# Skip projection of the nodes moved from the node stage into the edge stage, with a new order of the second norm and the sum with x

## The reference

```
h    = relu(layernorm(x))
z    = layernorm(h) * ln1_g + ln1_b
q, k, v = z @ Wq.T + bq, z @ Wk.T + bk, z @ Wv.T + bv        (4 heads of 32)
e    = edge_attr @ We.T
a    = softmax over the edges of one target of (q[dst] . (k[src] + e)) / sqrt(32)
out  = segment_sum(a * (v[src] + e), dst)
skip = z @ Wskip.T + bskip                                   (one row per node)
beta = sigmoid([out, skip, out - skip] @ Wbeta.T)
x_l  = h + beta * skip + (1 - beta) * out
h2   = layernorm(x_l) * ln2_g + ln2_b
x1   = x + x_l + relu(h2 @ W1.T + b1) @ W2.T + b2            (hidden width 512)
```

## Time and profile before

| | us |
|---|---|
| median of 3 runs | 3551.7 |
| the profiled execution, its own time | 3547.84 |
| its span, first to last instruction | 3546.1 |
| mean granted TensorE clock (1.00 is 2.4 GHz) | 0.837 |
| busy: TensorE / VectorE / ScalarE / GpSimd | 2276.2 / 2282.9 / 1725.3 / 2351.8 |

### The profile page before, as it was taken

One profiled execution on the slowest core, in us unless ns is written; L12 is line 12 of the kernel. 1 busy time (PEld: TensorE's weight loads), 2 busy tenths in 40 slices (PEclk: granted clock), 3 DMA queues, 4 the chain that ended last, 5 costly groups with the idle time before them and its releaser, 6 DMA issues. The chain is left out here.

```text
span 3546.1 us, 56764 instructions
## 1 busy us (share of the span) xinstructions
PE 2276.2 (64%) x13730; PEld 1826.3 (52%) x13730; DVE 2282.9 (64%) x9173; ACT 1725.3 (49%) x4075; POOL 2351.8 (66%) x2429
## 2 busy tenths in 40 slices
PE   0002887877877774799999999996444343455554
PEld 0002777777766672566666666664333332444444
DVE  8886666666666664678878878884111111677777
ACT  8994233332333332588888888885111111343433
POOL 5554777777777771665565556562777775777776
PEclk9999999999999995899999999998555555555555
DMA  6553233333333332233333434441666664556676
GB/s 204 177 177 94 83 101 91 91 101 91 91 101 92 91 101 63 70 109 102 111 106 102 106 104 108 101 104 67 130 131 128 132 130 103 130 142 146 145 153 124
DMA packets 253889, 401.94 MB, mean 113 GB/s; under 512 B 56515, under 2 KB 165456, under 8 KB 253728
## 3 DMA queue, kind: packets, MB, share of 16 engines
q1 hardware_dynamic: 183670, 265.77, 25.5%
q0 software_dynamic: 63424, 133.57, 19.7%
q10 hardware_dynamic: 6682, 1.46, 0.3%
HBM read 241.74 MB, written 160.29 MB: 113 GB/s over the span
## 5 line engine op out<-in xcount | busy, mean ns | idle before, releaser
L1159 POOL DMA_INDIRECT agg<-rows,at_n x392 | 393.8, 1005 | 149.6 <-issue 116.3
L1657 POOL DMA_INDIRECT aggc<-rows,at_nc x392 | 406.1, 1036 | 113.2 <-issue 104.8
L628 POOL DMA_INDIRECT zs<-z_table,at_s x392 | 381.3, 973 | 112.9 <-issue 102.5
L628 POOL DMA_INDIRECT zd<-z_table,at_d x392 | 374.0, 954 | 119.4 <-issue 110.9
L1482 POOL DMA_INDIRECT h2s<-h_table,at_s x392 | 373.3, 952 | 113.2 <-issue 90.2
L1535 PE MATMUL p_sum<-h2s,same 128*128 128x129 f32 x784 | 206.3, 439 | 310.8 <-DMA h2s<-h_table,at_s 206.6
L1233 PE MATMUL p_f<-w_t,act 128*128 128x128 f32 x3136 | 383.8, 278 | 0.0
L1222 PE MATMUL p_f<-z_t,w_t 128*128 128x512 f32 x784 | 374.9, 612 | 4.3 <-ACT act L1294 4.1
L1233 PEld LDWEIGHTS p_f<-w_t,act 128*128 128x128 f32 x3136 | 361.2, 192 | 22.2 <-issue 22.2
L1535 PEld LDWEIGHTS p_sum<-h2s,same 128*128 128x128 f32 x784 | 174.6, 323 | 342.4 <-issue 275.3
L1522 DVE TENSOR_SCALAR same<-dst_sb,dst_g 128x128 f32<-128x128 uint16 x392 | 83.9, 302 | 404.1 <-DMA dst_sb<-dst 370.5
(11 more groups left out here) (317 smaller groups left out, 6444.7 us busy)
## 6 DMA issues: line engine op xcount, KB each, us to landing
rows<-rows_sb SPq DMA_DIRECT2D x49, 576.0 KB
h_table<-h2b SPq DMA_DIRECT2D x49, 516.0 KB, 2.9
rows<-rows_sb SPq DMA_DIRECT2D x49, 516.0 KB
xa<-in_x_dram SPq DMA_DIRECT2D x49, 512.0 KB, 3.7
z_table<-za SPq DMA_DIRECT2D x49, 512.0 KB, 2.9
dst_sb<-dst SPq DMA_DIRECT2D x98, 256.0 KB
xb<-in_x_dram SPq DMA_DIRECT2D x49, 512.0 KB, 4.0
x_table<-x1b SPq DMA_DIRECT2D x49, 512.0 KB
```

The source lines that it names most:

```text
L628: pool.indirect_dma_start(out=to[:, slot, k], out_offset=None, in_=z_table, in_offset=bass.IndirectOffsetOnAxis(ap=at[:, slot, k:k + 1], a ...
L1159: pool.indirect_dma_start(out=agg[:, ring, k], out_offset=None, in_=rows0, in_offset=bass.IndirectOffsetOnAxis(ap=at_n[:, ring, k:k + 1], ...
L1657: pool.indirect_dma_start(out=agg[:, slot, k], out_offset=None, in_=rows1, in_offset=bass.IndirectOffsetOnAxis(ap=at_n[:, slot, k:k + 1], ...
```

## The change

The projection leaves the node stage. The edge stage loads 8 tiles of z rows of nodes per step (`zn`), turns them in pairs (bank p_tr[1]; the gathered rows share p_tr[0] alone), multiplies by wsk_t in the bank of v (p_v), copies the result out and stores it in `skip_table`. The node stage loads it with x. In the banks that come free the node stage has two for z2 and four for f1. The prep chain (den, recip, wa_sum, now with one logit add) moves behind norm2 on VectorE; x_xl moves behind norm2 too; the eighth tile of z2 goes from ScalarE to VectorE; gate_exp and the copies of z2 come first on ScalarE, and h2 and h are in another order. The diff, cut to its core:

```
@@ edge stage, SyncE @@
                         if new:
                             g, slot, use = new
+                            at_least(sp, node_turned, 4 * (g - 1))
+                            hold(sp, held)
+                            rows = z_table[bass.ds(first_row(g), GR), :].rearrange("(p t) d -> p t d", t=G)
+                            sp.dma_start(zn[:, slot], rows).then_inc(zn_in[slot], 16)
                             at_least(sp, same_ready, 4 * (g - 1))
...
                             sp.dma_start(rows, rows_sb[:, slot]).then_inc(stored[slot], 16)
+                            if isinstance(g, int) and g == NGN - 1:
+                                sp.wait_ge(skip_out[1 - slot], 16 * ((g - 1) // 2 + 1))
+                            sp.wait_ge(skip_kept, 4 * g + 4)
+                            hold(sp, held)
+                            rows = skip_table[bass.ds(first_row(g), GR), :].rearrange("(p t) d -> p t d", t=G)
+                            sp.dma_start(rows, skip_sb[:, slot]).then_inc(skip_out[slot], 16)
@@ edge stage, TensorE @@
+                    def turn_nodes(g, slot, use, n):
+                        if n == 0:
+                            pe.wait_ge(zn_in[slot], 16 * (use + 1))
+                        at_least(pe, node_copied, 4 * g + n)
+                        hold(pe, held)
+                        for k in range(2):
+                            last = t_.transpose(p_tr[1][:, k * P:(k + 1) * P], zn[:, slot, 2 * n + k], ident[:])
+                        last.then_inc(node_turned, 1)
+
+                    def skips(g, slot, use, n):
+                        pe.wait_ge(node_copied, 4 * g + n + 1)
+                        pe.wait_ge(v_copied, 4 * g + n + 1)
+                        hold(pe, held)
+                        for k in range(2):
+                            last = t_.matmul(p_skip[:, k * (D + 1):(k + 1) * (D + 1)], zn_t[:, n % 2, k], wsk_t[:], start=True, stop=True)
+                        last.then_inc(node_skipped, 1)
 # turn:
-                        at_least(pe, z_copied, 4 * g + u - 1)
+                        at_least(pe, z_copied, 4 * g + u)
 # project, before the value part:
+                        at_least(pe, skip_kept, 4 * g + u)
 # half:
                         if new:
+                            turn_nodes(*new, 0)
                             turn(*new, 1)
                             project(*new, 0)
...
                         if new:
+                            skips(*new, 0)
+                            turn_nodes(*new, 1)
                             turn(*new, 2)
                             project(*new, 1)
...
                             add_up(*old, 3)
+                        if new:
+                            skips(*new, 3)
@@ edge stage, ScalarE: copy_nodes before copy_z, keep_skip after each skips @@
+                        a.activation(zn_t[:, n % 2].rearrange("p a b -> p (a b)"), p_tr[1][:, 0:2 * P], ACT.Copy, bias=1.0).then_inc(node_copied, 1)
+                        a.activation(skip_sb[:, slot, 2 * n:2 * n + 2], p_skip.rearrange("p (t c) -> p t c", t=2), ACT.Copy).then_inc(skip_kept, 1)
@@ node stage, SyncE, behind the load of x @@
+                            rows = skip_table[bass.ds(first_row(g), GR), :].rearrange("(p t) d -> p t d", t=G)
+                            sp.dma_start(skip_sb[:, ring], rows).then_inc(skip_in[ring], 16)
@@ node stage, TensorE @@
-                            at_least(pe, S["f1_copied"], 8 * g + 4 * q + c - 1)
-                            t_.matmul(p_f1[c % 2][:, :], w1_t[:, c * P:(c + 1) * P], z2_t[:, q].rearrange("p a b -> p (a b)"),
+                            at_least(pe, S["f1_copied"], 8 * g + 4 * q + c - 3)
+                            t_.matmul(p_f1[c][:, :], w1_t[:, c * P:(c + 1) * P], z2_t[:, q].rearrange("p a b -> p (a b)"),
...
                         if mlp:
-                            turn_z2(mlp[0], mlp[1], 0)
-                        if gating:
-                            skips(gating[0], 0)
...
+                            for q in range(2):
+                                turn_z2(mlp[0], mlp[1], q)
+                            for q in range(2):
+                                up(mlp[0], q)
+                            for q in range(2):
+                                down(mlp[0], q)
@@ node stage, VectorE: the z_sb loop (L1364) and the three logit adds (L1374) go; then @@
                             v.tensor_scalar(var2[:], mv2[:, :, 1], EPS, None, ALU.add).then_inc(S["var2"], 1)
-                            v.tensor_tensor(x_xl[:, ring], x_l[:, slot], x_sb[:, ring], ALU.add).then_inc(S["xxl_ready"], 1)
...
                             v.scalar_tensor_tensor(norm2[:, slot, 1], mv2[:, :, 0], -1.0, norm2[:, slot, 0], ALU.mult, ALU.mult).then_inc(S["norm2_ready"], 1)
+                            v.tensor_tensor(x_xl[:, ring], x_l[:, slot], x_sb[:, ring], ALU.add).then_inc(S["xxl_ready"], 1)
+                            dve.wait_ge(S["norm2_ready"], g + 1)
+                            at_least(dve, S["z2_turned"], 2 * g)
+                            v.tensor_scalar(z2[:, G - 1], x_l[:, slot, G - 1], norm2[:, slot, 0, G - 1:G], norm2[:, slot, 1, G - 1:G], ALU.mult, ALU.add).then_inc(S["z2_more"], 1)
+                        if prep:
+ # den, recip, wa_prod, wa_sum as before, then
+                            dve.wait_ge(skip_in[ring], 16 * (lap + 1))
+                            at_least(dve, S["gate_exp"], g - 1)
+                            v.tensor_tensor(logit[:, slot], skip_sb[:, ring, :, D], wa_sum[:], ALU.add).then_inc(S["logit_ready"], 1)
```

More of the change, by code:

```diff
@@ L604, in build @@
             at_ready, deg_done = s("at_ready"), s("deg_done")
+            zn_in, skip_out = ([s(f"e0_{n}{a}") for a in range(2)] for n in ("zn_in", "skip_out"))
+            node_turned, node_copied, node_skipped, skip_kept = (s(n) for n in ("node_turned", "node_copied", "node_skipped", "skip_kept"))
             wea1 = t("wea1", [META, D + DV])
@@ L738, in half @@
                         if new:
+                            skips(*new, 1)
+                            turn_nodes(*new, 2)
                             turn(*new, 3)
@@ L744, in half @@
                         if new:
+                            skips(*new, 2)
+                            turn_nodes(*new, 3)
                             project(*new, 3)
@@ L782, in half @@
                         if new:
+                            copy_nodes(*new, 0)
                             copy_z(*new, 1)
@@ L793, in half @@
                         for u in (0, 1, 2):
+                            if new:
+                                keep_skip(*new, u)
+                                copy_nodes(*new, u + 1)
                             if new and u < 2:
@@ L801, in half @@
                             copy_sums(*old, 3)
+                        if new:
+                            keep_skip(*new, 3)
                     act.wait_ge(zeroed, 2)
@@ L1220, in up, with down @@
                         for c in range(4):
-                            at_least(pe, S["f1_copied"], 8 * g + 4 * q + c - 1)
-                            t_.matmul(p_f1[c % 2][:, :], w1_t[:, c * P:(c + 1) * P], z2_t[:, q].rearrange("p a b -> p (a b)"),
+                            at_least(pe, S["f1_copied"], 8 * g + 4 * q + c - 3)
+                            t_.matmul(p_f1[c][:, :], w1_t[:, c * P:(c + 1) * P], z2_t[:, q].rearrange("p a b -> p (a b)"),
                                       start=True, stop=True).then_inc(S["f1_done"], 1)
-                    def down(g, q, tiles):
-                        if 0 in tiles:
-                            at_least(pe, S["y_ready"], 2 * (g - 1) + q + 1)
-                            pe.wait_ge(S["f1_copied"], 8 * g + 4 * q + 4)
-                            hold(pe, held)
-                            t_.matmul(p_f2[q][:, :], ones3[:], b2_parts[:], start=True, stop=False)
-                        for k in tiles:
+                    def down(g, q):
+                        at_least(pe, S["y_ready"], 2 * (g - 1) + q + 1)
+                        pe.wait_ge(S["f1_copied"], 8 * g + 4 * q + 4)
+                        hold(pe, held)
+                        t_.matmul(p_f2[q][:, :], ones3[:], b2_parts[:], start=True, stop=False)
+                        for k in range(4):
@@ L1277, in z2_of @@
                         at_least(act, S["z2_turned"], 2 * (g - 1) + q + 1)
-                        for k in range(4 * q, 4 * q + 4):
+                        for k in range(4 * q, 4 * q + 4 - q):
                             last = a.activation(z2[:, k], x_l[:, slot, k], ACT.Identity, bias=norm2[:, slot, 1, k:k + 1], scale=norm2[:, slot, 0, k:k + 1])
@@ L1321, in half @@
                                 if last and c % 2 == 1:
-                                    h2_of(last[0], last[1], last[2], (4 + 2 * q + c // 2,))
+                                    h2_of(last[0], last[1], last[2], (2 + 2 * q + c // 2,))
+                        if last:
```

(9 more changed lines are left out.)

153 lines of the change are left out of this document (53 added, 100 removed).

## The result

The changed kernel takes 3864.73 us (median, 3857.25 to 3878.24) where the one before takes 3549.27 (3542.35 to 3558.76) on the same chip: ratio 1.0891, 95% interval 1.0851 to 1.0931. It is slower, as forecast, but by 315 us and not by 153, and outside the range. The profiled span is 3855.5 us against 3546.1, 309 more.

What follows compares the result with a forecast made beforehand. The prediction took GpSimd's gathers to pace the edge stage and GpSimd's loop the node stage. Span 3546.1 + 268 (edge) - 115 (node) = 3699 us, 3705 us as measured time; range 3590 to 3840.

Steps and rivals of the forecast that it cites:

- What paces: Edge stage becomes a loop of add_up, stores, node load and turns, 26.0 us a step; GpSimd's loop paces the node stage.
- Issue of the load: Edge stage: SyncE issues the node load 2.43 us after the last add_up, behind two stores.
- Landing: Edge stage: the node load takes 5.0 us from issue to landing, bounds 3.2 and 7.0.
- late load: Rival, edge stage: the load lands at 7.0 us behind the stores, +94 us, 3799 us; chance 0.21.
- TensorE's work, 17.1 us: Edge stage: TensorE needs 17.1 us from the first node transposes to the end of the last add_up.
- Clock, 1.5 us: Edge stage: a slow TensorE clock after the new wait loses 1.5 us a step, bounds 0 and 3.
- Shared bank p_v at 0: Edge stage: waits from v and skip products sharing a bank cost 0; upper bound 2.3 us a step.
- Node stage, 17.9 us forecast: Node step 20.29 to 17.9: var2 wait -4.10, power -0.86, norm2 to var3 +2.6, gathers unchanged; -115 us in all.
- TensorE's full relief: Rival, node stage: the step falls to TensorE's own 16.6 us, 62 us more gain, 3643 us; chance 0.17.
- The other side: Rival, edge stage: the load comes early enough to cost nothing, so the change wins 115 us, 3437 us; chance 0.12.

Runs made afterwards that it cites:

- e2: Changed kernel with the node load issued behind the wait for the old sums but ahead of both stores; 3645.07 us, ratio 1.0279.
- e3: Changed kernel with the node load issued between the store of rows0 and the store of the skip rows; 3775.64 us, ratio 1.0647.
- e4: Changed kernel plus sixty unused identity transposes before TensorE's wait for the node load; 3785.23 us, ratio 1.0675.
- e1: Changed kernel with the edge stage's node load issued one step ahead, before the wait for the old sums; 3487.82 us, ratio 0.9849.
- e5: Kernel of e1 with x_xl moved back behind var2 in the node stage; 4134.88 us, ratio 0.9543, on another chip.
- e6: Kernel of e5 with the prep chain also moved behind var3; 4106.19 us, ratio 0.9421, on the chip of e5.
- e10: Kernel of e1 with the prep chain moved behind var3 and x_xl left behind norm2; 4156.82 us, ratio 0.9432, on another chip.
- e11: Kernel of e5 with a second sum of the same size right behind x_xl; 4166.77 us, ratio 0.9448, on the chip of e10.

## Why the prediction was wrong in size and right in kind

**What paces.** Right. The change made a loop of SyncE's wait, two stores and the node load; GpSimd's gathers now wait for turns, and the node stage runs by GpSimd's loop.

**Issue of the load.** Right: 2.43 us forecast, 2.48 measured in the step shown and 2.3 on the mean.

**Landing: the step that failed.** I took 5.0 us between 3.2 and 7.0, by the median of a load with one store ahead and the 6.16 us of the earlier trace rows. Measured is 7.13 in the step shown and 7.0 on the mean of 47. The "late load" rival, with 7.0, had the right term, and its 3799 us lacks the other misses below. e2 and e3 show the reason: 4.3, 5.5, 7.0 us on the mean with none, one and two stores ahead. I had named the two stores and then priced the load by rows with at most one. The term is worth 2.0 x 47 = 94 us, more than half of the 160 us by which the forecast was short.

The Trainium skill, "DMA: Bandwidth & Descriptors", section "Two DMAs through the same engine are not ordered", has descriptors of a queue start in order, and e2 and e3 agree. The estimate by its "Anatomy of one DMA" was 5.8 us from the first store's issue to the landing; the trace has 1020.74 - 1011.83 = 8.9. That section's fit is for single transfers that GpSimd issues, and these three are queued by SyncE, so the estimate used it beyond what it states. The measurement decides: with the engines 89% busy, 257 GB/s were moved, not the 436 of the estimate.

**TensorE's work, 17.1 us.** Right: 17.35 on the mean in e4, where no slow clock is left.

**Clock, 1.5 us.** 2.1 by e4, another 0.6 x 47 = 28 us. The term was also read from a stretch that isn't the one right behind the wait: from 901.5 to 903 us the clock was still 0.94, and the 0.50 of the earlier trace rows came after it.

**Shared bank p_v at 0.** Right on the chips of the result and of e1: e1 leaves 0.2 us a step (10 us) for everything that was added, and in the changed kernel the profile lists no wait of TensorE for a copy of v or of the skip rows from 600 to 1600 us, only the two kinds in the result's waits. On the chips of e5, e6, e10 and e11, where ScalarE's copy is late, TensorE does wait for it.

The sum of a held edge step: 2.3 + 7.0 + 17.35 + 2.1 = 28.7 us, measured 28.7, forecast 26.0. (Against the forecast's 47 x 5.7 = 268 us the stage lost 384.)

**Node stage, 17.9 us forecast, 18.67 measured.** Of its four terms two held: the power -0.82 (forecast -0.86), and what now stands between norm2 and var3, 3.75 - 44.8/39 = +2.60 (forecast +2.6; the 44.8 us in 39 steps is the wait for var3 in the trace before, in the stretch of the earlier trace rows). The other two are the miss of 0.8: the wait for var2 went from 4.10 to 0.58, not to 0, since in 12 steps of 49 it is still late; in front of L1369 VectorE has 8 idles of 3.0 us each (24.1 us in all) that no releaser explains, and what makes them is open; and gathers, at which I had put no change, grew from 1009 to 1050 ns on the mean, 0.33 us a step. With the two, 20.29 - 0.82 + 2.60 - 3.52 + 0.33 = 18.9 us, 0.2 above the measured step. The rows of the trace before, from 1500 to 2300 us:

```profile
L1159 POOL DMA_INDIRECT agg<-rows,at_n x311 | 313.7, 1009 | 119.6 <-issue 92.2 <-POOL at_n L1167 27.5
...
POOL norm L1181 <- DVE var L1440: 44.8, 39, 1.3
```

Two gathers of the trace after, each with VectorE's first base product beside it; the first starts late in the product, the second at its start:

```profile
2172.73 1.23 DVE L1384 TENSOR_TENSOR base<-agg,keep 128x1024 f32<-128x1024 f32 x1
...
2173.62 1.16 POOL L1220 DMA_INDIRECT agg<-rows,at_n  x1 [0.30 <-issue]
...
2190.51 1.22 DVE L1384 TENSOR_TENSOR base<-agg,keep 128x1024 f32<-128x1024 f32 x1
...
2190.57 1.98 POOL L1220 DMA_INDIRECT agg<-rows,at_n  x1 [0.30 <-issue]
```

The kernel before had such gathers too, but only 4 over 1.9 us; the changed one has 25. A faster step shifts VectorE's long products against GpSimd's gathers, and more of them now start together. TensorE's full relief (3643 us) did not come, as the loop forecast.

**The other side** asked for a landing within 3.2 us of add_up. Even e2, the best place behind the wait, has 0.9 to the issue and 4.3 to the use, 5.2 together. Ahead of the wait it comes about: e1's 3487.82 us is faster than before, by 58 us (3545.54 in that comparison) and not by the 115 that the rival counted, because the node stage gave 78 and the edge stage still costs 10.

## What to carry to other kernels

A load that is new in a step and stands behind the wait for the step before can make the step a loop of wait, issue, landing and work, as here (28.7 instead of 20.3 us); issued ahead of that wait it cost 0.2 us a step in e1. Look first at what the issuing queue is blocked on, then at what it has in front. Price a landing by rows with the same transfers queued ahead, not by the median of a load like it. And a VectorE instruction moved out of one engine's way can land in another's: ask which gather or power will start beside it.

## What was not expected of the hardware

- A load of 0.5 MB: 4.3, 5.5 and 7.0 us from issue to use, on the mean, behind none, one and two stores of 516 to 576 KB on the same queue.
- A GpSimd gather that starts inside a VectorE sum or product of 128x1024 ends 0.8 to 0.9 us behind its end, so it takes up to 2.00 us instead of 0.94; one that is already under way takes 0.94 to 0.95. The power that starts inside such a sum takes up to 2.6 us instead of 1.64.
- The kernel before took 3546 to 3549 us in three comparisons and 4334.92 and 4411.58 us in two others, on other chips. With the early load the edge stage steps in 31.0 to 31.6 us on those two and in 20.4 to 20.5 on the others, with ScalarE's copy of v late for a reason that is open. The ratios of e5, e6, e10 and e11 hold for those two chips only, and e1's account of the edge stage for the others only.
